# Both chunks of a new unit of W's second half added up on GpSimd, and one pass of VectorE moved behind the first tile

## The reference

```python
w = weights[subjects]
x1 = jnp.einsum('bct,bcd->bdt', x, w)                       # _L0_cond_ref
result = jnp.einsum('bnd,od->bno', x1, W_base) + b_base     # _L0_ffn_ref
logits = jnp.einsum('bnd,ed->bne', x1, W_gate)
probs = jax.nn.softmax(logits.astype(jnp.float32), axis=-1)
top_p, top_i = jax.lax.top_k(probs, TOP_K)
top_p = top_p / jnp.sum(top_p, axis=-1, keepdims=True)
route_w = jnp.sum(jax.nn.one_hot(top_i, E, dtype=x.dtype) * top_p[..., None], axis=-2)
h = jnp.einsum('bnd,erd->bner', x1, A)
delta = jnp.einsum('bner,eor->bno', h * route_w[..., None], B)
return x + result + delta * SCALING
```

## Time and profile before

| | |
|---|---|
| median of 3 runs | 1579.23 us (1577.51 to 1581.52) |
| the profiled execution | 1579.12 us, of which span 1577.3 us |
| PE busy | 1506.0 us (95%) |
| DVE busy | 1352.3 us (86%) |
| POOL busy | 640.5 us (41%) |
| ACT busy | 626.1 us (40%) |
| chain that ended last | PE 73%, DVE 11%, issue 4%, POOL 2% |

### The profile page before, as it was taken

One profiled execution on the slowest core, in us unless ns is written; L12 is line 12 of the kernel. 1 busy time (PEld: TensorE's weight loads), 2 busy tenths in 40 slices (PEclk: granted clock), 3 DMA queues, 4 the chain that ended last, 5 costly groups with the idle time before them and its releaser, 6 DMA issues.

```text
span 1577.3 us, 25817 instructions
## 1 busy us (share of the span) xinstructions
PE 1506.0 (95%) x9411; PEld 808.5 (51%) x9411; DVE 1352.3 (86%) x2257; ACT 626.1 (40%) x1026; POOL 640.5 (41%) x508
## 2 busy tenths in 40 slices
PE   4678999999999999999989999999999999999998
PEld 4554554555455555555545455555455555455553
DVE  6788999999899999999968888888888888888875
ACT  6864444444543445434413332223332323332321
POOL 2565555666665555665522122122122122122122
PEclk9899999999999999999999999999999999999999
DMA  6234555655555555655797333344333344433342
GB/s 232 94 132 156 163 165 173 191 166 161 150 176 167 161 168 178 177 179 157 227 339 247 108 123 101 99 141 126 116 121 91 111 141 123 118 116 94 114 111 74
DMA packets 169567, 235.95 MB, mean 150 GB/s; under 512 B 71898, under 2 KB 88794, under 8 KB 167130
## 3 DMA queue, kind: packets, MB, share of 16 engines
q1 hardware_dynamic: 167426, 219.63, 46.0%
q10 hardware_dynamic: 2016, 14.68, 2.4%
HBM read 147.83 MB, written 86.43 MB: 149 GB/s over the span
## 4 chain that ended last, share of the span: by engine, by line
PE 73%; DVE 11%; issue 4%; POOL 2%; DMA 1%; ACT 1%; SPq 0%; DVEq 0%; ACTq 0%; POOLq 0%
PE bank_x L1427 8%; PE bank_x L1429 8%; PE bank_x L1428 8%; PE bank_y L1427 8%; PE bank_y L1429 8%; PE bank_y L1428 8%; PE bank_z L1427 3%; PE bank_z L1429 3%; PE bank_z L1428 3%; PE bank_h L1427 2%; PE bank_h L1429 2%; PE bank_h L1428 2%; PE bank_c L1427 2%; DVE t_sums L1070 2%; PE bank_c L1429 2%
## 5 line engine op out<-in xcount | busy, mean ns | idle before, releaser
L602 POOL TENSOR_TENSOR x_res<-x_res,t_sums 128x512 f32<-128x512 f32 x255 | 350.5, 1377 | 843.4 <-DVE t_sums L1075 684.1
L1427 PE MATMUL bank_y<-TT,s_parts 128*128 128x512 f16 x768 | 292.1, 380 | 4.7 <-DVE TT L1185 4.2
L1427 PE MATMUL bank_x<-TT,s_parts 128*128 128x512 f16 x768 | 292.9, 381 | 1.3 <-DVE TT L1185 1.3
L1428 PE MATMUL bank_x<-TT,s_parts 128*128 128x512 f16 x768 | 292.5, 381 | 0.0
L1429 PE MATMUL bank_x<-TT,s_parts 128*128 128x512 f16 x768 | 292.3, 381 | 0.0
L1429 PE MATMUL bank_y<-TT,s_parts 128*128 128x512 f16 x768 | 291.9, 380 | 0.0
L1428 PE MATMUL bank_y<-TT,s_parts 128*128 128x512 f16 x768 | 291.9, 380 | 0.0
L710 ACT ACTIVATE p_copies<-bank_x,y_inv 128x512 f32<-128x512 f32 x128 | 87.7, 685 | 417.7 <-PE bank_x L1429 307.3
L1075 DVE TENSOR_TENSOR t_sums<-t_sums,inv_w 128x512 f32<-128x512 f32 x255 | 233.8, 917 | 8.7
L1045 DVE TENSOR_TENSOR s_parts<-a_full,s_parts 128x512 f16<-128x512 f32 x224 | 192.9, 878 | 33.0 <-ACT s_parts L695 33.0
L574 POOL TENSOR_TENSOR x_res<-x_res,BT 128x512 f32<-128x512 f32 x128 | 206.9, 1616 | 26.3 <-DMA x_res<-in_x_dram 23.3
(11 more groups left out here) (243 smaller groups left out, 2750.5 us busy)
## 6 DMA issues: line engine op xcount, KB each, us to landing
x<-in_x_dram SPq DMA_DIRECT2D x32, 1024.0 KB, 5.8
x_res<-in_x_dram SPq DMA_DIRECT2D x128, 256.0 KB, 4.0
part_scratch<-x_res SPq DMA_DIRECT2D x128, 256.0 KB, 3.0
x_res<-part_scratch SPq DMA_DIRECT2D x128, 256.0 KB, 3.9
out_dram<-x_res SPq DMA_DIRECT2D x128, 256.0 KB, 3.0
wt_scratch<-late_words SPq DMA_DIRECT2D x64, 224.0 KB, 3.4
TT<-wt_scratch ACTq DMA_DIRECT2D x14, 1024.0 KB, 8.3
x_parts<-in_L_ffn_W_base_dram SPq DMA_DIRECT2D x18, 512.0 KB, 6.4
```

The lines of the kernel that those rows point to most:

```text
L602: nc.gpsimd.tensor_tensor(XR[:, xr_slot(m), :], XR[:, xr_slot(m), :], TM[:, m % 2, :], ALU.add).then_inc(r_added, 1)
L1427: nc.tensor.matmul(dst, lhs[0], rhs[0], start=start, stop=False, skip_group_check=chained)
L1428: nc.tensor.matmul(dst, lhs[0], rhs[1], start=False, stop=False, skip_group_check=chained)
```

## The change

The sums of chunk 0 move from DVE to POOL in the eight steps that begin a unit, `on_vector` and `n_sums` keep the counts of the two semaphores right, and `lower_chunk` of chunk 0 moves on DVE from ahead of `finish(n, 0, C11)` to behind it. In the steps with chunks 2 and 3 nothing moves. In step 7 all four chunks are now added up on POOL, the first three ahead of the bias.

```diff
+        def on_vector(g, c):
+            return c == 2 and g != WHOLE
+
+        def n_sums(g, c, vector):
+
+            return len([1 for u in range(g + 1) for k in range(C4) if (u, k) <= (g, c) and on_vector(u, k) == vector])
@@ POOL
-                    for c in chunks[1:3]:
-                        add_up(g, c)
+                    for c in chunks[0:3]:
+                        if not on_vector(g, c):
+                            add_up(g, c)
                     add_bias(8 * n + begin)
@@ ACT, upper_chunk
-                first_chunks = [(unit, chunks[0]) for unit, chunks in WINDOWS]
-                if (g, c) in first_chunks:
-                    act.wait_ge(bg_sum_first, n_window(g, c))
+                if on_vector(g, c):
+                    act.wait_ge(bg_sum_first, n_sums(g, c, True))
                 else:
-                    act.wait_ge(bg_sum, n_chunk(g, c) - n_window(g, c))
+                    act.wait_ge(bg_sum, n_sums(g, c, False))
@@ DVE
-                if chunks:
+                if chunks and on_vector(g, chunks[0]):
                     add_up_first(g, chunks[0])
                 if not second:
                     find_top(n + 1)
@@ DVE
-                if chunks:
+                if chunks and on_vector(g, chunks[0]):
                     lower_chunk(g, chunks[0])
                 finish(n, 0, C11)
+                if chunks and not on_vector(g, chunks[0]):
+                    lower_chunk(g, chunks[0])
                 if more:
                     scale_x(n + 1)
```

## The result

| | before | after |
|---|---|---|
| median | 1579.61 us (1577.51 to 1581.52, 4 runs) | 1595.49 us (1592.74 to 1599.43, 4 runs) |
| the profiled execution, its span | 1579.12, 1577.3 us | 1595.79, 1593.9 us |

The ratio of the times is 1.0104, interval 1.0091 to 1.0117: slower, by about 16 us, as forecast. The parts of the sum did not all come out as forecast.

What follows compares the result with a forecast made beforehand. PE's work plus its waits bound the kernel. Five steps at 2.2 us, two at 1.7 and step 7 at 2.0 sum to 16.4 us on 1579.12: 1595.5 us, range 1585 to 1599.

Steps and rivals of the forecast that it cites:

- What bounds: PE, busy 95% of the span, plus its waits; the repeating one, ahead of the first `cond`, totals 8.3 us.
- Relief of DVE at C11: In step 3 C11 starts at 242.46, 1.41 us earlier; `lower_chunk` behind it costs 1.01, leaving a gain of 0.40.
- Four operations of POOL ahead of L1038: In steps 3, 5, 10, 12, 14 queued biases and `add_r` hold up DVE's passes: PE goes on 2.2 us later each.
- Steps 1 and 8: DVE's passes come earlier against POOL's queue, the last bias may fall behind L1038: 1.0 to 2.3, taken 1.7 us each.
- Step 7: Turn of chunk 3 on PE 2.0 us later, as ACT's copy of chunk 2 waits for the moved `lower_chunk`; no lock.
- Nothing of this is given back later: Claim that the added delays all stay in the time, since PE has no slack to catch up with.
- The first `cond` idle: Sign of being right: in steps 3, 5, 10, 12, 14 PE idles about 3.1 us there behind L1038, now 1.03.
- L1036 and L1038 of 2.3 and 1.3 us: Sign of being right: these DVE passes last that long, L1038 or L1036 of about 1.3 and 2.3, in five steps.
- a sign of being wrong: In those five steps L1036 and L1038 at 1.28 and 0.34 us as now, or POOL's third bias over before them.
- A: Rival: not slower, POOL's backlog fits beside other work; 1575.4 us if L1038 ends under 251.4 in step 3; chance 0.12.
- B: Rival: one operation of POOL fewer gets ahead of L1038 in each of seven steps; 7.5 us more, 1586.6 us; chance 0.18.
- C: Rival: more than forecast, step 7's next `cond` delayed again and seams against DVE elsewhere; 21 us more, 1600 us; chance 0.10.

Runs made afterwards that it cites:

- experiment 2: Kernel before, with only `lower_chunk` of chunk 0 moved behind C11 in the steps that begin a unit: 1582.44 us, ratio 1.0028.
- experiment 4: Kernel after, with chunk 0's four subtractions on POOL replaced by one operation of 128x4: 1582.98 us, ratio 1.003.
- experiment 12: Kernel after with step 7 as before and POOL's biases 7 and 8 placed beside DVE's search for the maxima: 1577.35 us, ratio 0.9988.
- experiment 3: Kernel after, but in step 7 chunk 0 is added up on DVE and its `lower_chunk` stands ahead of C11: 1589.30 us, ratio 1.0068.
- experiment 11: Kernel before, with POOL's biases 7 and 8 placed beside DVE's search for the maxima: 1574.41 us, ratio 0.9975.

## Why the prediction was right, and where it was not

- **What bounds.** Right: the waits of PE ahead of `cond`, behind L1038, and at the turn of chunk 3.
- **Relief of DVE at C11.** Right as a start (242.46 in experiment 2; C11 starts 0.11 us behind `spread_maxima` in the kernel after), and right that it would not pay. Its worth ahead of `scale_x`, 0.40 us by my working, was eaten by the bias beside L1075 (experiments 2 and 4: a step stays at 44.17 and 44.16 us).
- **Four operations of POOL ahead of L1038.** The mechanism is right: experiment 4 takes the 1.25 us away, experiment 12 takes it away in another way. The size was off: 10.34 us from `spread_maxima` to `cond`, where the sum gave 253.6 - 242.36 = 11.24. The eight subtractions are over 1.11 us behind `spread_maxima` (246.68), forecast 1.44: 0.33. They no longer meet DVE's sums, and each lasts 0.46 us where two of the old four lasted 0.50. From there to the end of L1046 it takes 9.18 us, forecast 9.91 less the 0.18 I took off for seams: 0.55. The mis-sized term is mostly those seams. Instructions overlap by 0.07 to 0.09 us where one pass of DVE follows the other, and that way has nine seams, between passes of both engines; 0.55 and the 0.18 already taken off make 0.08 us each. I had counted them as hundredths. So a step costs 1.25 us, five of them 6.3 in place of 11.0.
- **Steps 1 and 8.** Forecast 1.7 each. Step 8 takes 2.55 us more, in both executions. 0.9 us come from waits: the one ahead of `cond` is 1.07 us longer, and a delay of 0.15 ahead of `spread_maxima` is gone. That is under the 1.0 to 2.3 of my range, and the last bias did not fall behind L1038 (now L1046) but ahead of it. The other 1.65 us are the clock, below, which I had not in the sum. Step 1 follows the start-up and scatters by 1.6 us before and 2.5 after. The wait of 1.56 us that I took for it is one execution's; the second execution of the kernel before has 0.22. So its cost can't be told from two executions each.
- **Step 7.** The term for the turn was right, 2.07 of 2.0, and depends on no lock, as said. "Nothing of this is given back later" was wrong: shorter waits later in the step give back 1.4 and 1.1 us. In the first execution matmuls at half clock take 1.4, in the second none, so the step costs 1.8 us between the means. That the mean lies near 2.0 is luck. In the one trace with step 7 put back (experiment 3) step 8 keeps its clock.
- **The total.** 15.9 us measured between medians, 16.4 forecast. That is closer than the terms deserve: 4.7 us too much in five steps stand against some 4 us for the clock and for what scatters. That the clock would fall was in no case of mine. So the mechanism, POOL's queue against DVE's passes, was right, and that the total fits to 0.5 us is luck.
- **Signs.** As listed: eight subtractions in a row, biases of 1.8 us and more beside DVE's passes (3.79 for two, forecast "2 us and more"), C11 idle until product 2, the turn at 3.35, second halves unchanged. The first `cond` idle 2.29 us, not 3.1. L1036 and L1038 of 2.3 and 1.3 us: seen in step 8 (2.29 and 1.34), not in the five steps. There they last 1.27 and 0.34 and POOL's third bias is over (253.45) before them, which I had named a sign of being wrong. The sign was badly chosen: the sum needs four turns of POOL ahead of L1038, and they came two passes earlier, beside the two L1256.
- **Rivals.** A needed L1038 over earlier than now: it ended 1.3 us later (255.86 - 245.57 = 10.29 behind `spread_maxima`, 9.01 before). B (three turns of POOL instead of four, 1586.6): there were four, though a step's cost, 1.25, lies nearer to B's 0.93 than to my 2.2. C: seams went for DVE, not against it; its 1600 us did not come.

What stays open: whether the change has a part in the start-up and in steps 15 and 16, whose DMA waits differ between executions (the means in the table are 1.5 us apart), and how much of experiment 3's 5.7 us is the change's, since the traces show 3.8 and the error is 3.

## What to carry to other kernels

Work moved off the busier engine is free only if the idler one has no queue at that place: add up what stands behind the moved work there, and whether it meets passes of the other engine that exclude it. When each engine holds the other up, count turns, not busy shares, and take off the overlap at each seam (some 0.08 us here). A bias that depends on nothing but its DMA is best placed beside work that it does not hinder (here the search for the maxima, experiment 11), and held there by a wait rather than by its place in a list.

## What the runs showed of the hardware

**PE's clock after a long wait.** In steps 1 to 14 the granted clock fell to half only behind waits that the change had made longer; behind the start-up the kernel before has such a stretch in step 16 alone, of 13 matmuls of 128x512, behind a wait of 4.68 us (2.76 us in its second execution). PE's timeline of the kernel after in step 8 and the same stretch by windows (the clock is the number ahead of the last two):

```profile
485.70 0.25 PE L1437 MATMUL bank_c<-w_cond_parts,x_parts 128*128 128x128 f16 x1 [2.62 <-DVE w_cond_parts L1046]
...
486.91 0.63 PE L1437 MATMUL bank_x<-TT,s_parts 128*128 128x512 f16 x1
487.33 0.63 PE L1438 MATMUL bank_x<-TT,s_parts 128*128 128x512 f16 x1
```
```profile
485.70:490.00 4.30, 4.30 (x22) 2.43 (x23) 2.75 (x4) 1.23 (x2) 1.37 (x2) 0.60 0.54 152
490.00:495.00 5.00, 5.00 (x43) 3.00 (x42) 4.10 (x5) 2.13 (x4) 3.66 (x3) 1.00 0.90 336
```

The matmuls stand 0.42 us apart, 0.22 at full clock: the two levels are 1.2 and 2.4 GHz. It costs 1.65 us here. The same happened after the 2.29 us in step 3 (0.43 us apart from 257.39 on), but in one of two executions only, and after 3.35 us in step 7, for 5 matmuls of 128x512 in one execution of the kernel after, none in the other and 12 in experiment 2. It did not happen in step 8 of experiment 3:

```profile
481.40 0.23 PE L1437 MATMUL bank_c<-w_cond_parts,x_parts 128*128 128x128 f16 x1 [2.60 <-DVE w_cond_parts L1046]
```

The wait is the same to 0.02 us, and all matmuls behind it keep their 0.22. So the length of the wait alone does not decide it; what else does I did not isolate. None of the waits ahead of `cond` in the kernel before, up to 1.6 us, was followed by it. The Trainium skill (TensorE: Matmul & The Clock Gate, the part on the HAM clock gate) says that the moment of a change of clock varies from run to run of one kernel. The two executions of step 3 agree, with 8 slow matmuls in one and none in the other.

**Turns between POOL and DVE.** The lock that the prediction described (the Trainium skill, SBUF — State Buffer, on the two separate sides of SBUF) shows in every timeline above: a pass that meets an operation of POOL lasts longer by what is left of that operation, up to about 1.0 us (2.15 and 2.13 in place of 1.09; 1.64 in place of 0.69). The prediction's list of such passes lacks its own first example, L1029 with one tensor as input: it lasts 1.11 us beside `add_r` and 0.17 in step 7, where no `add_r` meets it. In step 3 of the kernel after neither engine gets two turns in a row while the other waits: bias, L1256, bias, L1038, `add_r`, L1039, bias, L1256 is the order of the rows.
